# Two layers of attention and mixture of experts on one core: normalising during attention, the router between the shared products, dispatch in parts, early expert weights

## The reference

```python
# layer 0 and layer 1, each:
y = x + attention(layernorm(x), context)          # 16 heads of 16; windows of 128 (layer 0), 256 keys (layer 1)
n = layernorm(y)
# layer 0: 16 experts of 256, the best two per token by n @ router_w, gates = sigmoid
w_full[token, sel] += sigmoid(top_vals)
moe    = einsum('ne,nec->nc', w_full, (silu(gate) * up) @ down_w[e])
shared = (silu(n @ shared_gate.T) * (n @ shared_up.T)) @ shared_down.T
x = y + moe + shared
# layer 1: 8 experts of 1024 with relu and biases, the best two, softmax over the two
x = y + sum over the best two of g * (relu(n @ W1[e] + b1[e]) @ W2[e] + b2[e])
```

## Time and profile before

| | us |
|---|---|
| median of 3 runs (lowest to highest) | 1005.78 (1005.52 to 1007.23) |
| the profiled execution | 1005.06 |
| its span in the trace | 1003.2 |
| TensorE busy | 801.9 |
| VectorE busy | 614.6 |
| ScalarE busy | 383.0 |
| GpSimd busy | 232.1 |

### The profile page before, as it was taken

One profiled execution on the slowest core, in us unless ns is written; L12 is line 12 of the kernel. 1 busy time (PEld: TensorE's weight loads), 2 busy tenths in 40 slices (PEclk: granted clock), 3 DMA queues, 4 the chain that ended last, 5 costly groups with the idle time before them and its releaser, 6 DMA issues.

```text
span 1003.2 us, 23252 instructions
## 1 busy us (share of the span) xinstructions
PE 801.9 (80%) x8478; PEld 604.9 (60%) x8479; DVE 614.6 (61%) x1405; ACT 383.0 (38%) x753; POOL 232.1 (23%) x203
## 2 busy tenths in 40 slices
PE   5969996587797999997869999945106999999993
PEld 3535553544455878874525666635105999989992
DVE  4445774356744667767666888467784656556561
ACT  3324553132232222233315566635134444344440
POOL 1200000000001777761100000011002444444431
PEclk9987998578999999999976999965557999999997
DMA  8990000372245233327980000088062343433434
GB/s 254 104 126 4 3 3 25 129 264 68 92 133 187 88 98 100 104 89 203 114 105 5 3 2 3 3 308 283 1 214 80 70 76 65 73 69 70 73 61 110
DMA packets 74062, 96.77 MB, mean 96 GB/s; under 512 B 14384, under 2 KB 58288, under 8 KB 73968
## 3 DMA queue, kind: packets, MB, share of 16 engines
q1 hardware_dynamic: 58176, 64.26, 27.0%
q0 software_dynamic: 13872, 29.24, 11.7%
q10 hardware_dynamic: 1952, 2.39, 0.8%
HBM read 63.09 MB, written 19.92 MB: 83 GB/s over the span
## 4 chain that ended last, share of the span: by engine, by line
PE 64%; DVE 18%; DMA 7%; issue 5%; ACT 3%; POOL 1%; SPq 0%; DVEq 0%; POOLq 0%; ACTq 0%
PE bank L851 15%; PE bank L864 12%; PE bank L648 5%; PE bank L669 4%; PE bank L617 3%; PE bank L769 3%; PE bank L760 3%; PE bank L504 3%; PE bank L836 2%; PE bank L763 2%; PE bank L530 2%; DVE arena L1484 2%; PE bank L635 2%; DVE neg_max L1275 2%; PE bank L519 2%
## 5 line engine op out<-in xcount | busy, mean ns | idle before, releaser
L851 PE MATMUL bank<-arena 128*128 128x128 f16 x3024 | 304.7, 221 | 3.4 <-DVE arena L1489 3.4
L864 PE MATMUL bank<-arena 128*128 x1224 | 282.8, 275 | 4.7 <-DVE arena L1497 3.0
L851 PEld LDWEIGHTS bank<-arena 128*128 x3024 | 266.1, 99 | 20.3 <-issue 4.2
L1631 POOL DMA_INDIRECT arena<-xn_d,get_i x87 | 88.7, 1020 | 224.6 <-DVE arena L1484 179.3
L1143 ACT ACTIVATE arena<-bank,arena 128x128 f32<-128x128 f32 x312 | 86.7, 377 | 124.0 <-DMA arena<-in_exp_b 71.5
L1275 DVE TENSOR_REDUCE neg_max<-bank 128x2 f32<-128x512 f32 (+1 forms) x180 | 117.3, 685 | 27.4 <-PE bank L617 26.4
L864 PEld LDWEIGHTS bank<-arena 128*128 128x128 f16 x1224 | 120.1, 98 | 15.7 <-issue 13.0
L1026 ACT ACTIVATE arena<-bank 128x1024 f32<-128x1024 f32 x96 | 96.5, 1026 | 11.5 <-PE bank L635 11.3
L1641 POOL DMA_INDIRECT sum_d<-arena,put_i x39 | 63.1, 1617 | 111.3 <-DVE arena L1510 101.0
L1497 DVE TENSOR_TENSOR arena<-arena 128x512 f16<-128x512 f32 (+1 forms) x126 | 74.8, 593 | 4.3
L836 PE MATMUL bank<-consts,arena 128*128 128x128 f32 x174 | 35.9, 291 | 44.4 <-DVE arena L1484 34.2
(11 more groups left out here) (171 smaller groups left out, 1130.8 us busy)
## 6 DMA issues: line engine op xcount, KB each, us to landing
arena<-arena SPq DMA_DIRECT2D x96, 128.0 KB, 6.5
arena<-in_exp_up SPq DMA_DIRECT2D x16, 512.0 KB, 3.8
arena<-in_exp_up SPq DMA_DIRECT2D x5, 1024.0 KB, 5.8
arena<-in_exp_dn SPq DMA_DIRECT2D x5, 1024.0 KB, 8.0
arena<-in_exp_b SPq DMA_DIRECT2D x39, 128.0 KB, 3.0
arena<-in_ctxT SPq DMA_DIRECT2D x8, 512.0 KB, 6.9
xn_d<-xn_buf POOLq DMA_DIRECT2D x8, 512.0 KB, 4.9
arena<-in_exp_dn SPq DMA_DIRECT2D x16, 256.0 KB, 4.0
```

What stands on the lines that cost most here:

```text
L851: last = mm(upP[u][:, m // (UB // 2), m % (UB // 2) * P:(m % (UB // 2) + 1) * P], weights(e, 0, w, k * UPW[l] + m * P, P), rowsT[u][x][:, ...
L864: last = mm(yP[u], hidT[u][x][:, k], weights(e, 1, w, k * D, D), start=n == 0, stop=n == n_second - 1)
L1631: pool.indirect_dma_start(rows[i % 2], None, xn_d[l], bass.IndirectOffsetOnAxis(ap=get_i[:, i:i + 1], axis=0)).then_inc(s["rows_in"][i % 2 ...
```

## The change

- In `attend`, VectorE measures each tile's statistics two blocks behind (`measure`, L1353), makes mean and variance of tiles 0 to 11 in block 14 and scales them (`apply`, L1357) in block 15. Only chunk 3 is left for the router. All four chunks have a buffer each (`xn_all`), and chunk 0 is turned before the last block's own turn.
- In `route`, TensorE scores a chunk and turns the next; in layer 0 the copy goes straight into `xnT_all` and SP's DMA is gone. The first pair of the shared part stands between the scores of chunks 2 and 3.
- In layer 0 the parts of dispatch and inverse stand between the shared part's products on VectorE, as do the cuts.
- POOL issues the shared part's weights and expert pieces 0 to 4 before the first attention's end (pieces 0 to 2 at once, 3 and 4 as buffers come free); pieces 0 and 1 are cut in blocks 12 and 13. SP loads the other eleven.
- In the first projection chunk 3 is turned ahead of the queries of chunk 2, and ScalarE issues the first shift row's DMA in SP's place.

```diff
@@ projection of layer 0, TensorE
                         values(c)
+                        if c == NC - 2:
+                            turn_tokens(NC - 1, 1)
                         queries(c, c % 2)
-                    turn_tokens(NC - 1, 1)
@@ VectorE, step of attend
+                    if left > 1:
+                        measure(early_stats[:, ds(i - 2, 1)].rearrange("p o n -> p (o n)"), i - 2)
+                    else:
+                        measure(stats[:, 1 - left], i - 2)
+                    if l == 0 and isinstance(i, int) and 12 <= i < 12 + FIRST0:
+                        cut_low(0, i - 12)
...
+                    if left == 0:
+                        chain.n += 1
+                        dve.wait_ge(s["sd_ready"], NC + 1)
+                        chain.then(v.reciprocal(early_rstd, early_std))
+                        for c in range(NC - 1):
+                            apply(c, early_mean_var[:, c * TC:(c + 1) * TC], early_rstd[:, c * TC:(c + 1) * TC])
+                            if c == 0:
+                                divide(T - 1)
@@ TensorE, route
+                for c in range(NC):
+                    score(c, c % 2)
+                    if l == 0 and c == NC - 2:
+                        shared_up(0, 0)
+                    if c + 1 < NC:
+                        turn_normal(l, c + 1)
@@ VectorE, dispatch of layer 0
+                    dve.wait_ge(s["xn_kept"], NC * 16)
...
-                    shared(0, 0)
+                    cut_low(0, FIRST0)
+                    shared_hidden(0, 1)
+                    cut_low(0, FIRST0 + 1)
+                    shared_hidden(0, 2)
+                    cut_low(0, FIRST0 + 2)
...
+                    shared_hidden(0, 3)
+                    cut_low(0, FIRST0 + 3)
...
+                    shared_add(0)
+                    shared_hidden(1, 0)
+                    cut_low(0, FIRST0 + 4)
@@ GpSimd
+                if l == 0:
+                    pool.wait_ge(s["tr_mm"], NC)
+                    pool.dma_start(sh_gate, a["sh_gate"].rearrange("(k p) n -> p k n", p=P)).then_inc(sh["w_in"], 16)
+                    pool.dma_start(sh_up, a["sh_up"].rearrange("(k p) n -> p k n", p=P)).then_inc(sh["w_in"], 16)
+                    pool.wait_ge(s["q_mm"], NC)
+                    pool.dma_start(sh_down, a["sh_down"].rearrange("(k p) n -> p k n", p=P)).then_inc(sh["w_in"], 16)
+                    pool.wait_ge(once["far_in"], 2 * 16)
+                    for q in range(3 + FIRST0):
+                        after(pool, s["w_lo"], q - 2)
+                        load_piece0(pool, q, s["w_early"])
```

More of the change, by code:

```diff
@@ L229, in block_sems @@
                 s["hid_v"] = sem("hid_v_0")
+                s["w_early"] = [sem(f"w_early{u}_0") for u in range(3)]
             else:
@@ L314, in stacked, with place_shift, load_piece0 @@
                     eng.wait_ge(s_in[u], ((c - u) // 2 + 1) * STACKS * 16)
+        def place_shift(queue, l, i):
+            s = B[l]
+            queue.wait_ge(s["nm_ready"], i + 1)
+            for g in range(2):
+                queue.dma_start(q_stack[64 * g + KR:64 * g + KR + 1, :, ds(i * P, P)],
+                                neg_maxT[8 * g:8 * g + 8]).then_inc(s["shift_in"], 16)
+        def load_piece0(queue, q, s_in):
+            first, e = KD * UPW[0], ORDER[0][q]
+            queue.dma_start(staged[0][q][:, 0:first].rearrange("p (k n) -> p k n", k=KD),
+                            a["exp_up0"][e].rearrange("(k p) n -> p k n", p=P)).then_inc(s_in[q % 3], 16)
+            queue.dma_start(staged[0][q][:, first:WCOL[0]].rearrange("p (k n) -> p k n", k=HK[0]),
+                            a["exp_dn0"][e].rearrange("(k p) n -> p k n", p=P)).then_inc(s_in[q % 3], 16)
         W_IN, WQK_IN = 5 * 16, 3 * 16
@@ L917, in _ @@
                 if l == 0:
-                    shared(0, 0)
-                dispatch(l)
-                if l == 0:
-                    for c in range(1, NC):
-                        shared(c, c % 2)
+                    for c in range(NC):
+                        for m in range(1 if c == 0 else 0, SHB):
+                            shared_up(c, m)
+                            if c == 0 and m == 2:
+                                dispatch(0)
                         if c == NC - 2:
                             invert(0)
+                        shared_down(c, c % 2)
                 else:
+                    dispatch(1)
                     invert(1)
@@ L994, in project @@
                         values(c)
+                        if c == NC - 2:
+                            turned(NC - 1, 1)
+                        if c == NC - 1:
+                            place_shift(act, l, 0)
                         queries(c)
@@ new lines, in step @@
+                    if left == 1:
+                        chain.n = EARLY + 1
+                        dve.wait_ge(chain.sem, chain.start + chain.n)
+                        for t in range(EARLY):
+                            last = v.bn_aggr(early_mean_var[:, t], early_stats[:, t])
+                        chain.then(last)
+                        v.tensor_scalar(early_var, early_mean_var[:, :, 1], EPS, None, ALU.add).then_inc(s["var_ready"], 1)
+                    if left == 0:
[4 more added lines that the diff above has]
+                            apply(c, early_mean_var[:, c * TC:(c + 1) * TC], early_rstd[:, c * TC:(c + 1) * TC])
+                            if c == 0:
+                                divide(T - 1)
@@ L1312, in attend, with measure, apply @@
+                def measure(to, i):
+                    dve.wait_ge(s["x_att"], i + 1)
+                    v.bn_stats(to, x_res[:, ds(i, 1)].rearrange("p o d -> p (o d)")).then_inc(chain.sem, 1)
+                def apply(c, of, r):
+                    for t in range(TC):
+                        last = v.tensor_scalar(xn_all[c][:, t], x_res[:, c * TC + t], of[:, t, 0:1], r[:, t:t + 1], ALU.subtract, ALU.mult)
+                    last.then_inc(s["xn_ready"], 1)
                 maxima(1, 1, 0, NM)
@@ L1313, in attend @@
                 dve.wait_ge(s["bo_added"], NC)
-                in_all_pairs(dve, T, step)
-                divide(T - 1)
+                in_all_pairs(dve, T, step, 2)
                 add(T - 1)
+                measure(stats[:, 2], T - 2)
+                measure(stats[:, 3], T - 1)
+                chain.n += 2
+                dve.wait_ge(chain.sem, chain.start + chain.n)
+                for t in range(TC):
+                    last = v.bn_aggr(mean_var[:, t], stats[:, t])
+                chain.then(last)
@@ L1353, in dispatch @@
                 chain = own[l]
+                hot1, hot2, hot, cnt, run0, run1 = hots[l]
+                over, le = over2[l], le2[l]
                 by_e = lambda x: x.rearrange("p (t o) -> p t o", o=1).to_broadcast([P, T, E])
@@ L1583, in _ @@
                 if l == 0:
-                    for c in range(1, NC):
-                        shared(c, c % 2)
-                        if c == 1:
-                            inverse(0)
-                        if c == NC - 2:
-                            inverse_read(0)
+                    inverse(0)
+                    shared_hidden(2, 2)
+                    cut_low(0, FIRST0 + 10)
+                    shared_hidden(2, 3)
+                    shared_add(2)
+                    shared_hidden(3, 0)
+                    inverse_read(0)
+                    cut_low(0, FIRST0 + 11)
+                    shared_hidden(3, 1)
+                    cut_low(0, FIRST0 + 12)
+                    shared_hidden(3, 2)
+                    cut_low(0, FIRST0 + 13)
+                    shared_hidden(3, 3)
+                    shared_add(3)
                 else:
```

265 lines of the change are left out of this document (135 added, 130 removed).

## The result

| us | before | after |
|---|---|---|
| median (lowest to highest) | 1005.65 (1002.88 to 1007.23), 4 runs | 974.37 (969.76 to 979.21), 4 runs |
| the profiled execution, its span | 1005.06, 1003.2 | 979.21, 977.4 |
| last sum of attention 0 | 166.87 | 182.21 |
| from there to the start of the shared part's last sum | 147.8 | 118.9 |
| from there to the last sum of attention 1 | 340.9 | 341.8 |

The ratio is 0.969 (0.965 to 0.974): faster by 31 us. The profiled execution of after was the slowest of its four, so the columns, which are of two single executions, differ by 26 only. The first answer is the windows by stage, as in the earlier trace rows: attention 0 from its first sum, router 0, shared part and router 1.

The account below looks back on a forecast made before the run. TensorE, busy for 80% of the span, leaves 20% to win, mainly its waits for VectorE; 3.0 + 2.2 + 1.3 - 23.9 - 13.2 + 1.3 = -29.3 from 1005.06 gave 975.8, so 976 us, range 959 to 991.

Parts of the forecast that it names:

- The start: First projection and first blocks: late turn, earlier shift row and early weight loads together cost a net 3 us more.
- The 2 us that ScalarE's queue was to give back: Block 0's scores: the shift row, behind no restacking DMA on ScalarE's queue, would end a 2.01 us wait.
- Block 1's row: Shift row at the start of attention 0: delayed by early weight loads beside the restacking, 4 us taken between 0 and 9.
- Rival B: Early weights starve the shift rows of blocks 1 to 3, losing 9 to 20 us: 981 to 992 us, chance 0.17.
- Attention: First layer's attention: statistics cost nothing, two early cuts 2.2 us, the turn of chunk 0 1.3 us.
- First router: Layer 0's router: a chain of scores, turns, copies and the first pair, at cold clock, taking 24.7 us.
- Rival A: Warm first router: clock stays up, 8.9 us less there and no restarts, 964 us; chance with mixtures above 957: 0.22.
- Shared part: Last score to last down product: TensorE work 83.2 us plus waits for VectorE of 12.9, so 96.1, plus 3 for restarts.
- Rival D: VectorE's pieces in the shared part collide more, each wait twice as long: 990 us, chance 0.10.
- Second router: Layer 1's router: last best two 27 us behind the last sum, in place of 40.23, so 13.2 us less.
- The formula 7.4 + 5.4 k: Second router: estimated landing time in us of weight piece k, four 1 MB pieces sharing DMA with 4 MB of stores.
- Rival C: Attention falls to half clock, 3 us more per block, slower than before from some ten blocks; 1018 us, chance 0.03.

Follow-up runs that it names:

- a2_again: The changed kernel run again, unaltered: 974.57 us (970.72 to 984.27, 6 runs).
- e1_late: Changed kernel with the early loads of shared weights and pieces 0 to 2 held until block 1's sum, all at once: 974.43 us.
- e4_pair: Changed kernel with early loads spread one per block, plus the shared part's first pair one score earlier: 969.87 us, against 968.47 with the spread alone.
- e9_whole: Changed kernel with early loads spread one per block, plus the dispatch in one piece behind chunk 0's sum: 971.39 us, against 968.47 with the spread alone.
- e6_l1copy: Changed kernel with early loads spread one per block, plus ScalarE's copies ahead of cuts in layer 1's router: 967.47 us, against 968.47 with the spread alone.

## Why the prediction was right, step by step

The forecast of 976 us stands 1.6 above the median. Some of that is luck: against the profiled execution the sum was 3.4 too low, and two terms were off by more, with opposite signs.

**The start: +3.0 forecast, +10.3 measured** in the profile (+9.4 in that of a2_again). This is the term that was mis-sized: 1.7 of it stand ahead of block 0's scores, for -1, and 8.5 ahead of block 1's, for 4. The turn's wait came as said: the first maxima are 1.3 us later, for 1.0. The 2 us that ScalarE's queue was to give back did not come: the row was issued at 62.65, behind no restacking of its own queue, and was there at about 74.5 all the same. Nor did it come sooner with the loads later: there block 0's scores start at 72.2 to 74.2, and before at 72.92. Block 1's row cost 8.54 us, where I took 4 between 0 and 9. The upper end had been worked out as a backlog that ends at 87 in place of 76; it ended a little after 87. The wait was 8.54 and 8.43 us in two executions, and at most 0.84 once the loads were later (e1_late). The section of the Trainium skill that I put beside it ("DMA: Bandwidth & Descriptors", Issuing engines are not separate DMA queues) says that the DMAs of all issuing engines share the same 16 engines, which put the value near the upper end; the trace agrees. Rival B was thus half true. It starved one block and not three, since the loads of 3.8 MB were through by then.

**Attention: +3.5 forecast, +5.0 measured.** The statistics cost nothing, as said: the blocks that have only them take 5.29 to 5.48 us, and before 5.38 to 5.48. The two cuts were put at 2.2 (0 to 3.5) and cost 3.2 in this profile (18.2 us, for 15.0, from the sum of block 11 to that of block 14) and 6.3 in that of a2_again, where the clock fell as well. The wait behind the first cut came at its size (1.36 us, for 1.4); the second was 1.58, for 0.8: block 14 has no maxima, so TensorE too has less work there (no L605 between L623 and the turn back) to cover the cut. That the row of shifts is then late at the last block's scores (0.92 at 172.25) stood nowhere in my working. The last block is 0.85 longer, not 1.3: a wait covers most of the turn of chunk 0. The other 1.1 us lie between the first two sums (7.40 us, before 6.28), behind block 1's late row.

**First router: 24.7 forecast to the last score's end, 20.8 measured** (203.00 less 182.21); in the other profiled executions with this order it was 20.8 to 23.5. (The terms that I listed add up to 24.6.) The two rows for it, full clock in the attention and half in the second router, were the two ends; I chose cold all through. The run was warm for two scores, cold for one score and most of the pair, and warm again. Behind the attention the clock stayed up for two scores and their turns and was then lost, and e4_pair shows it lost again behind a pair. The page "TensorE: Matmul & The Clock Gate" of the Trainium skill (Part 1, What's actually happening) says that activity releases the throttle; that rule and the row that I set against it are each right for a part of the stretch. Rival A held for half of the router.

**Shared part: 99.1 forecast (96.1 and 3 of restarts), 98.1 measured.** The waits were forecast as 3.6, 5.3, 3.4 and 0.6, and are 2.16, 4.96, 2.57 (inverse and product) and 0.78: 10.5 for 12.9. The cold restarts were 3.7 for 3. The order of VectorE's queue, written out piece by piece, gave each wait its place; e9_whole, worked out in the same way, came at its 7 us (7.15) as well. Rival D is out. Only one wait lies in the 3 to 6 us that I had named as the sign for three of them.

**Second router: 27 forecast, 27.5 measured**, near the arrival of the pieces as said (0.98 and 356 GB/s of DMA in it); e6_l1copy took 1.5 us off by the order of the copies. The formula 7.4 + 5.4 k gives 23.6 for the last piece, where I wrote 22; in e6_l1copy it was there 20.2 us behind the last sum. The stores of the normalised tokens delayed nothing. Rival C (attention at half clock) did not come as a whole: 0.92, before 0.93. A piece of it did, in a place that I had not thought of, where the clock fell behind the early cuts.

In sum, measured on the profiles: 10.3 + 5.0 - 28.9 + 0.9 - 12.7 - 0.4 = -25.8, for a forecast of -29.3. Why the median fell by 31 is not settled: e1_late shows that the 8.5 us of the start, so clear in two profiles, are not in the median at that size, and two things of the clock fall differently in each execution: its return in attention 1 (5 to 7 us) and its fall behind the early cuts (some 3 us).

## What to carry to other kernels

Where two engines hand buffers to each other in pairs, write out the queue of the one that is waited for and put work that nobody waits for behind the last product that somebody does: six cuts moved by one or two places were worth 5 us, splitting a 12 us dispatch about 1 in its stretch. A piece of 1.75 us in the wrong place can cost more than its own length: two of them cost 3.2 us where the clock held and 6.3 where it fell behind them. Loads put into a quiet stretch must still leave room for a small transfer that is waited for every 5 us; one large transfer for each block was 6 us better in the median than the same bytes in a burst, of which the profiles explain 1.5. And when two single executions are compared by stages, look at the granted clock in the stages that the edit does not touch: here they alone differed by 7 us.

## What the runs showed of the hardware that was not expected

- A 2 KB transfer beside the restacking of SP, at a DMA share of 1.16, took about 10 us from SP's own queue (before: issued at 63.3, block 0's scores at 72.92) and about 10 from an otherwise idle one (ScalarE's in e4_pair: 62.8, 72.81); with the early loads beside it as well it took about 12 (62.65 to 74.5).
- In the first attention the granted clock fell to half behind waits of TensorE of about 1.4 us in six of eight profiled executions, and a stretch of three blocks then took 19.0 to 21.6 us in place of 18.2 and 18.4; with the cuts in a gap (three executions) it took 14.9 and the clock stayed full.
- In the second attention the clock came back about 17 us after its fall in three profiled executions and 31 to 34 us in nine, with the same instructions from the projection on; what decides it is not shown.
- In the first router the granted clock was full until about 188 us, through two scores and two turns, then half, with TensorE busy 2.89 of 4 us in either stretch; it came back at about 198, in the wide pair that began at 193.00. In the second router it stayed at half with TensorE busy throughout.
- The changed kernel's profiled executions (979.21 and 984.27) were the slowest of their sets of 4 and 6, while e1_late's (969.91) was the fastest.
